# Reordering the start of the self-attention: unit 0's row maxima and sequence 1's projections in a one-core block kernel

## The reference

```
x = x + tanh(g_xattn[1]) * L1_xattn(layernorm(x), ctx)
# inside L1_xattn, NH = 16 heads of HD = 8, x = 0.1 * input:
nx = ln(x) * g_ln1 + b_ln1
q, k, v = nx @ W_sq + b_sq, nx @ W_sk + b_sk, nx @ W_sv + b_sv
s = q @ k.T * HD ** -0.5            # per head, 512 x 512
so = softmax(s) @ v @ W_so + b_so
```

## Time and profile before

| what | value |
| --- | --- |
| median of 3 runs | 463.72 us |
| the profiled execution's own time | 462.69 us |
| its span, first to last instruction | 460.9 us |
| PE busy in the span | 354.5 us, 77% |
| DVE busy in the span | 264.5 us, 57% |
| ACT busy in the span | 201.7 us, 44% |
| mean granted TensorE clock | 0.885 |

### The profile page before, as it was taken

How to read it: one execution, slowest core, us unless ns; L and a number is a source line. 1 busy time by engine, 2 the same in 40 slices (tenths; PEclk the granted TensorE clock), 3 DMA queues, 4 the chain that set the end, 5 groups by cost and what they waited for, 6 DMA issues and landing times.

```text
span 460.9 us, 6703 instructions
## 1 busy us (share of the span) xinstructions
PE 354.5 (77%) x2495; PEld 209.4 (45%) x2495; DVE 264.5 (57%) x661; ACT 201.7 (44%) x317; POOL 114.1 (25%) x155
## 2 busy tenths in 40 slices
PE   1797302995189899899999799987873899989970
PEld 0576301995133322233221467554463443677850
DVE  5425500332687598788950758544568947883435
ACT  2332100321040477677778458564624335565210
POOL 2000277156050716311110000010000055462232
PEclk9997555998579999999999779999995799899987
DMA  4599114001326656000000000001999467431232
GB/s 113 152 192 320 46 52 117 13 33 40 105 63 181 143 144 160 1 3 2 2 2 2 0 0 1 1 1 36 371 329 290 148 201 248 152 106 37 60 82 46
DMA packets 35876, 46.01 MB, mean 100 GB/s; under 512 B 4778, under 2 KB 21682, under 8 KB 35844
## 3 DMA queue, kind: packets, MB, share of 16 engines
q1 hardware_dynamic: 33156, 38.57, 29.9%
q0 software_dynamic: 2688, 7.02, 5.3%
HBM read 31.67 MB, written 13.78 MB: 99 GB/s over the span
## 4 chain that ended last, share of the span: by engine, by line
PE 58%; DVE 15%; issue 8%; ACT 6%; DMA 6%; POOL 5%; SPq 1%; POOLq 0%; DVEq 0%; ACTq 0%
PE ps L1397 9%; PE ps L1605 6%; PE ps L1591 5%; PE ps L1566 4%; PE ps L1851 4%; PE ps L1515 3%; PE ps L1574 3%; PE ps L1696 3%; PE ps L1880 3%; DVE early L1210 3%; PE ps L1527 2%; POOL disp_d L538 2%; PE ps L1801 2%; DVE xn L982 2%; PE ps L1786 2%
## 5 line engine op out<-in xcount | busy, mean ns | idle before, releaser
L1210 DVE TENSOR_REDUCE early<-ps 128x1 f32<-128x512 f32 x128 | 81.0, 684 | 15.9 <-PE ps L1566 11.7
L755 ACT ACTIVATE R<-ps 128x1024 f32<-128x1024 f32 x64 | 62.7, 1020 | 24.7 <-PE ps L1591 23.7
L1397 PE MATMUL ps<-ident,R 128*77 128x128 f32 (+1 forms) x224 | 35.3, 296 | 31.8 <-DMA R<-disp_d 24.8
L1397 PEld LDWEIGHTS ps<-ident,R 128*77 128x77 f32 (+1 forms) x224 | 26.7, 152 | 50.4 <-DMA R<-disp_d 25.2
L1566 PE MATMUL ps<-R 72*128 72x512 bf16 x112 | 39.0, 382 | 1.1 <-DVE early L1210 0.2
L1591 PE MATMUL ps<-R 75*128 75x512 bf16 x128 | 37.6, 379 | 1.6 <-DMA R<-R 1.3
L621 POOL DMA_INDIRECT R<-h_d,srow x16 | 16.5, 1033 | 77.3 <-DMA h_d<-ff 70.3
L1605 PE MATMUL ps<-R,vaug 128*9 128x512 f32 x256 | 33.5, 595 | 0.6 <-ACT R L755 0.6
L1179 DVE TENSOR_SCALAR R<-ps,vcol 128x256 f32<-128x256 f32 x16 | 7.0, 479 | 37.7 <-PE ps L1515 37.7
L1566 PEld LDWEIGHTS ps<-R 72*128 72x128 bf16 x112 | 10.8, 96 | 33.1 <-DVE early L1210 23.9
L538 POOL DMA_INDIRECT disp_d<-R,srow x16 | 15.9, 993 | 36.7 <-DVE srow L1125 32.1
(11 more groups left out here) (324 smaller groups left out, 696.2 us busy)
## 6 DMA issues: line engine op xcount, KB each, us to landing
R<-in_L_ffn_W_dram SPq DMA_DIRECT2D x1, 6144.0 KB, 19.9
h_d<-R SPq DMA_DIRECT2D x12, 256.0 KB, 2.8
q_d<-R SPq DMA_DIRECT2D x24, 96.0 KB, 1.9
R<-k_d SPq DMA_DIRECT2D x24, 96.0 KB
R<-q_d SPq DMA_DIRECT2D x8, 288.0 KB
R<-in_L_ffn_w_dram SPq DMA_DIRECT2D x1, 2048.0 KB, 17.1
h_d<-ff SPq DMA_DIRECT2D x6, 256.0 KB, 2.5
disp_d<-R SPq DMA_DIRECT2D x1, 1032.0 KB, 12.8
```

The source lines that it names most:

```text
L755: s.activation(probs[idx % 4], ps[:, 2 * (idx % 2):2 * (idx % 2) + 2, :].rearrange("p b t -> p (b t)"), ACT.Exp, scale=QK_SCALE).then_inc( ...
L1210: v.tensor_reduce(mcol[:, u, col:col + 1], bank(ring_bank("row", n)), AX.X, ALU.max).then_inc(s1_max, 1)
L1397: return m.transpose(dst, src, ident[0:k, 0:k])
```

## The change

It has four parts. DVE: the scalings of sequence 1's four tiles leave the layer norm and stand behind the row maxima 2, 5, 8 and 11, and the value bias of sequence 0 behind maximum 16; the factors are still formed where they were. PE: row tiles 16 and 17 now stand ahead of `max_transpose(0)`; of sequence 1 the transposes stand right behind it, and the key, query and value projections behind the row tiles 19, 21 and 23. `spin` is left only behind tiles 24 to 27. The ring order follows. SP: `load_max(1)` stands in the middle of sequence 1's query stores.

```diff
-        ring_order = [("row", n) for n in range(MU)] + [("max", 0)] + [("row", n) for n in range(MU, LEAD)]
+        ring_order = [("row", n) for n in range(MU + 2)] + [("max", 0)] + [("row", n) for n in range(MU + 2, LEAD)]
...
             sp.wait_ge(q_parts, 2)
-            for hg in range(HG):
-                store_queries(1, hg)
+            store_queries(1, 0)
+            store_queries(1, 1)
             load_max(1)
+            store_queries(1, 2)
+            store_queries(1, 3)
...
-                    scale_of(x2, xn, 2, t // TB, again=True)
+                    scale_factors(2, t // TB, again=True)
+                    if t < TB:
+                        for tile in range(TB):
+                            scale_tile(x2, xn, tile, again=True)
...
-            add_value_bias(0)
+
             for n in range(LEAD):
                 row_max(n)
+                if n < MU and n % 3 == 2 and n // 3 < TB:
+                    scale_tile(x2, xn, TB + n // 3, again=True)
+                if n == MU:
+                    add_value_bias(0)
...
-            project_keys_queries(0)
+            transpose_tiles(xn, ln_out, 2 * T, ln_tp, [0])
+            project_heads(0, 0)
+            project_heads(0, 1)
             project_values(0)
             for r in range(MU):
                 first_row_tile(r)
+            score_row_tile(MU)
+            score_row_tile(MU + 1)
             max_transpose(0)
-            project_keys_queries(1)
-            project_values(1)
-            for n in range(MU, LEAD):
+
+            transpose_tiles(xn, ln_out, 2 * T, ln_tp, [1])
+            for n in range(MU + 2, LEAD):
                 score_row_tile(n)
-                spin(256)
+                if n == MU + 3:
+                    project_heads(1, 0)
+                elif n == MU + 5:
+                    project_heads(1, 1)
+                elif n == MU + 7:
+                    project_values(1)
+                elif n > MU + 7:
+                    spin(256)
```

More of the change, by code:

```diff
@@ L971, in stats, with scale_factors @@
                 v.tensor_scalar(var_eps[:, 0, half], mv[:, half, 1], LN_EPS, None, ALU.add).then_inc(ln_stats, 1)
-            def scale_of(src, dst, i, b, again=False):
+            def scale_factors(i, b, again=False):
                 half = slice(b * TB, (b + 1) * TB)
@@ L980, in scale_of, with scale_tile @@
                     me.link(v.tensor_scalar(rstds[:, :, half], rstds[:, :, half], 0.1, None, ALU.mult))
+            def scale_tile(src, dst, t, again=False):
+                v.tensor_scalar(dst[:, t, 0:D], src[:, t, :], mv[:, t, 0:1], rstds[:, int(again), t:t + 1],
+                                ALU.subtract, ALU.mult).then_inc(ln_out, 1)
+            def scale_of(src, dst, i, b, again=False):
+                scale_factors(i, b, again)
                 for t in range(b * TB, (b + 1) * TB):
-                    v.tensor_scalar(dst[:, t, 0:D], src[:, t, :], mv[:, t, 0:1], rstds[:, k - 1, t:t + 1],
-                                    ALU.subtract, ALU.mult).then_inc(ln_out, 1)
+                    scale_tile(src, dst, t, again)
             def layer_norm(src, dst, i, again=False):
@@ L1537, in project_values, with project_heads @@
                 ins.then_inc(v_mm, 1)
-            def project_keys_queries(b):
-                transpose_tiles(xn, ln_out, 2 * T, ln_tp, [b])
+            def project_heads(b, n):
                 pe.wait_ge(xT_ready, 4 + b + 1)
[L1542 to L1545, removed]
+                if b:
+                    pe.wait_ge(qk_ready, masked[3] if n else K_0)
+                m.matmul(bank(3 - n), wx_qk[:, 1 - n, :], xT[:, b * SEQ:(b + 1) * SEQ], start=True, stop=True).then_inc(qk_mm, 1)
             def ring_free(kind, k):
```

## The result

The changed kernel takes 470.44 us, median of 19 runs (465.94 to 474.62), against 464.7 (460.9 to 470.26, 19 runs) for the kernel before: ratio 1.0113 [1.0079, 1.0148]. The ratio leaves out runs over 1.5% above the fastest of their kernel, so it isn't the quotient of the two medians. By it the change costs 5.2 us, where 3.2 were forecast. The sign came as predicted; the median lies 0.6 above 469.8, the end of the range. The kernel before took 464.7 here, where the forecast had counted from 463.72 (three runs), so 1.0 of the distance to the forecast isn't the change's. The profiled execution took 467.92 us (span 466.1, clock 0.88) against 462.69 us: 5.2 more as well. That execution is one of the quicker ones, as its twin of before was, and none of the 19 had a higher mean granted clock (0.856 to 0.880), so most of them had more low clock than this profile shows.

What follows compares the result with a forecast made beforehand. The prediction took PE, busy 77% of the span, as leading the chain, with SP's queue order as second bound. Step 8 1.5 later plus 1.7 of low clock gave + 3.2, 466.9 us on the median; range over the cases 461.8 to 469.8.

Steps and rivals of the forecast that it cites:

- Part 1, maxima ahead of scalings: VectorE, unit 0's row maxima: no wait in the ring, no clock fall, the last maximum 3.8 us earlier.
- T: End of unit 0's last row maximum (maximum 15): forecast 146.1 against 149.87, bounds 145.9 and 149.9.
- Rival 3: Maxima don't come earlier, POOL holding the scalings and PE's clock falling: + 1.8 to + 3.2; chance within the others' shares.
- Part 2, hand-over: TensorE, tiles 16 to 27 with projections between: done at T + 7.3; by PE and DVE alone step 0 7.1 earlier.
- What holds step 0: `load_max(0)` queues behind sequence 0's packed loads, lands at 158.0: 2.5 kept of 7.1, PE idles 4.6, clock falls.
- Rival 1: Small loads don't queue: `load_max(0)` lands 1.7 after issue, step 8 4.4 earlier, 459.3; chance 0.1.
- Part 3, `load_max(1)` inside the stores: SyncE: six stores behind `load_max(1)` put sequence 1's packed loads 6.15 behind X, 2.2 later than before, bounds 0.3 and 4.4.
- X: Issue of `load_max(1)` on SP: forecast 165.2, bounds 163.3 and 167.5.
- Step 8: PE waits for `load_max(2)`, landing 15.7 after sequence 1's first packed load (15.0 to 16.3): starts at 187.05, 1.5 later.
- The clock behind step 8: TensorE's clock falls after that wait: 3.4 at half speed costs 1.7, bounds 0 and 3.4.
- Rival 2: Both shifts cancel: step 8 at 184.5, one clock fall of 1.7, + 0.7, 464.4; chance 0.28 with all within 0.5%.

Runs made afterwards that it cites:

- Number 3: Second try of the kernel before with only the move of `load_max(1)` into the middle of sequence 1's query stores: 470.46 against 466.43 us, 1.0111.
- number 2: First try of the kernel before with only the move of `load_max(1)` into the middle of sequence 1's query stores: 476.25 us, 1.0196.
- numbers 11: Kernel before with `load_max(0)` ahead of sequence 0's last packed load and `load_max(2)` behind sequence 1's first: 463.61 us, 1.0016.
- Number 13: As number 10, without spins, but `load_max(0)` ahead of sequence 0's last two packed loads: 454.22 against 461.63 us, 0.9819.
- number 1: The change with all query stores of sequence 1 ahead of `load_max(1)` again: 466.47 against 465.13 us, 1.0071.
- number 4: The change with 14 and 22 matmuls of no use ahead of the waits of steps 0 and 8: 466.18 us, 1.0061.
- 4 to 9: Includes two runs of the change with 15 and 33 matmuls of no use at steps 0 and 8: 468.16 us, 1.0146, then 464.37 us, 1.0064.
- number 10: The change, all sequence 1 query stores ahead of `load_max(1)`, `load_max(0)` ahead of sequence 0's last packed load, `load_max(2)` behind sequence 1's first: 459.17 us, 0.9906.
- number 7: The change, unaltered, run once more: 465.31 against 461.63 us, 1.0059.
- number 8: The change with all sequence 1 query stores ahead of `load_max(1)` and 15 matmuls of no use ahead of step 0: 463.66 us, 1.0003.
- number 14: The change with `load_max(0)` ahead of sequence 0's last two packed loads and `load_max(2)` behind sequence 1's first: 457.38 against 466.43 us, 0.9835.
- number 12: As number 10, with 8 matmuls of no use ahead of the wait of step 0: 455.34 against 461.63 us, 0.9827.
- numbers 9: The change with `load_max(2)` issued behind the first packed load of sequence 1 instead of the last: 465.14 us, 1.0031.

## Why the prediction was right in its mechanism and short in its size

*Part 1, maxima ahead of scalings: right.* T came 3.6 earlier in the stage (3.8 forecast), with one slow scaling, no wait in the ring and no fall of the clock. Rival 3 fell with it. But not all of the 3.6 is sure to be there in each execution. Number 3 has the old order and the same wait in the ring, and there no fall followed (L1576 is its `first_row_tile`):

```profile
137.38 11.40 PE L1576 MATMUL ps<-attnT,R 128*128 128x512 f32 x26 [1.88 <-DVE early L1212]
```

The 26 matmuls take 11.40, not the 13.09 of the earlier trace rows, and T is at 16.85. So 1.7 of the 3.6 were the fall, and the sentence of the prediction that a gap of 1.8 "was enough for 1.2 GHz" holds in numbers 2 and 11 and not in number 3.

*Part 2, hand-over: right.* The last tile was done 7.1 behind T (154.9 against 132.88 + 14.93; 7.3 forecast). Number 13, where no load is in the way, shows what the two parts are worth: step 0 at 22.01, 7.2 earlier.

*What holds step 0: right.* `load_max(0)` took 5.12 and held step 0 for 3.4. It went out 19.04 behind tile 0, as forecast (150.35 is 19.03), and landed at 25.46, 1.2 sooner than forecast; in the eight profiles with this order on VectorE, TensorE and ahead of it on SP (the change, numbers 1 and 4 to 9) it lands between 25.5 and 26.7, so that much is chance. The fall of the clock behind it came, and lasted 6.8 where 3.4 were counted. The Trainium skill, DMA: Bandwidth & Descriptors, section "Queues, rings and completion order", says that on each DMA engine the descriptors of a ring are consumed in order. The runs agree: the last DMA of the same load took 5.12 behind all the packed loads, 5.01 with one of them moved behind it (number 10) and 1.75 with two (number 13). Rival 1, small loads that don't queue, is out.

*Part 3, `load_max(1)` inside the stores: right, with some luck.* The packed loads came 6.25 behind X (6.15 forecast). X at 33.40 (33.9 forecast) has two errors that cancel in part: step 0 was 1.1 early, and from there to X it took 7.8 instead of 7.2, because the low stretch was twice as long as counted. Numbers 2 and 3 show that this edit alone makes the kernel slower, number 1 that without it the queue's part is gone.

*Step 8: the term that was too small.* "I allow 15.0 to 16.3 and take 15.7" from the first packed load to the landing. It took 17.8. The load's last DMA was issued at 180.25, as late as in the earlier trace rows, but the bulk ahead of it had begun 3.3 later, and it took 10.10. I had shortened the 16.3 of before, taking its tail for slack; in the seven profiles with the late start and the loads in this order (the change, numbers 2 to 7) the term lies between 15.2 and 17.8, and is 18.1 in the longest run of number 2, with no rule that I found. Why the same bytes take 15.2 in one execution and 17.8 in another stays open. So step 8 was 3.3 late, not 1.5: 2.1 more by this term, 0.4 less by the earlier packed loads. That is the larger part of the 3.3 by which the stage missed the forecast.

*The clock behind step 8: too small as well.* "A low stretch of 3.4 at half speed costs 1.7 (bounds 0 and 3.4)". The length was read from one fall, in tiles of f32 whose ring DVE also fed. The same profile had a longer one, right behind the stage, with PE busy for most of it (window of the kernel before):

```profile
259.60:269.80 10.20, 8.46 (x18) 4.36 (x18) 5.28 (x20) 4.42 (x6) 0.00 (x0) 0.50 0.00 0
```

With 10.2 as a possible length the bounds would have been wider from the start. The fall at step 8 of the change lasted 10.2 (from 186.8, of which the last 6.6 behind the start of step 8); steps 8 to 11 took 15.21 instead of 12.03, 3.2 more; in number 3 the loss is 4.8. With 3.3 for the landing and 3.2 for the clock the stage lost 6.5, against 1.5 + 1.7 = 3.2. The rest of the span gave 1.3 back.

In the repeated run (number 7) both terms were at their low ends, 15.2 and no fall, and the ratio of 1.0059 is inside what was forecast. Rival 2 (both shifts cancel) nearly stands there in the profile, 1.8 later in the stage. The interval of that set, [1.0019, 1.0098], overlaps the first one's, so the two sets don't differ for certain. The spread of the single runs doesn't help: it is 8.7 us with the change and 9.4 without.

What isn't settled: that the falls cost time is read in the stage (steps 8 to 11 take 15.21 or 16.79 with one and 12.03 without), and over the 19 runs of the change a lower mean clock goes with a longer time (correlation -0.7), but no pair of sets timed together shows the price of a single fall. Keeping PE busy takes the falls away but was no faster than the change where both were timed together (1.0064 and 1.0059), with spins that outlasted the landing by 2; spins that stop with the landing weren't tried. And stages and times differ: number 8 is 2.9 better in the stage than before and equal in its times; number 14 is 2.6 better than 12 and equal. In the profiles this is the part behind the stage, whose code is the same in all. It holds 50.0 of low clock in number 8 (44.3 before) and is 2.5 longer; it holds 41.2 in number 14 (36.7 in number 12) and is 3.6 longer. Whether an earlier end of the stage brings this about or chance does isn't shown.

## What to carry to other kernels

When an edit lets an engine arrive earlier, look at which small transfer it meets there, and what stands ahead of that transfer in the issuing engine's queue: here 7.2 us gained on VectorE and TensorE turned into a loss until two loads went ahead of bulk that nobody needed yet. An issue that is moved up for one reader moves everything behind it down; count the landings behind it to the last reader, not to the next, and price a wait on TensorE as its length plus the low clock behind it, unless a later wait hides that. Take the length of that low clock from all low stretches of the profile, not from the nearest.

## What the runs showed of the hardware that was not expected

- The low clock behind a wait lasted 3.4, 6.8, 10.2 or 13.7 us, though TensorE was busy in all of it, or in all but the first 3.6 and 3.3 that still lay in the wait (step 8 in the change and in number 3). It came with idle stretches of 1.7 (number 10), 2.1 (number 4), 3.4 and 6.2 us (the change), and 4.0 (number 7). A wait of 1.3 ahead of step 8 in the kernel before brought none, one of 1.3 ahead of step 4 in number 13 brought 3.4 of low clock, and one of 1.9 ahead of step 8 in number 8 brought none; the wait of 1.9 in the ring brought 3.4 in the kernel before and in numbers 2 and 11, and none in number 3. The length of the wait alone doesn't tell. The Trainium skill, TensorE: Matmul & The Clock Gate, section "HAM oscillation", puts some 1.67 us on one throttled stretch of the kernel that it describes; the stretches here are two to eight times that.
- Small loads of one shape took from 1.7 us on free engines to 10.10 us behind a bulk of packed loads (the change, ahead of step 8).
- A fetch of instructions can stand in the way of a small load too. With free engines ahead of it the last DMA of `load_max(2)` took 1.75 or 1.76 from issue to landing in numbers 9, 10, 13 and 14, and 2.70 and 3.28 in numbers 11 and 12, where the profile has one packet of the instruction queue (16 KB, about 1 us) at just that time. That the packet is the cause is inferred from the coincidence.
